# Softmax maxima 12 slots ahead instead of 16, and the routed experts two at a time over sixteen turns, in a fused two-layer kernel

## The chip, the cores and the metric

One NeuronCore of a Trainium2 chip runs the whole program. The metric is device time in microseconds (us) from start to end of one execution, as the median of several runs. Engines are named as the profile names them: PE (matrix), PEld (its weight loads), DVE (vector), ACT (scalar), POOL (GpSimd), SP (the engine that here only issues DMAs).

## The reference

Two layers over 16 batches of 512 tokens of 128 features. What matters here:

```python
# layer 0: test-time memory (a small MLP trained chunk by chunk), then
xc   = causal_conv3(layernorm(x)) ; q, k, v = xc @ wqkv          # full attention
att0 = softmax(q k^T / sqrt(8)) v         # 16 heads of 8 features, 512 x 512 each
x1   = layernorm(att0 @ wo + x)           # "z" below; then a dense mixture of 8 experts
# layer 1
a    = causal_attention(x)                # 16 heads of 8
b    = causal_attention(conv3(a))         # a second one on its result
# routed experts: 32, top 8 of a token, at most 128 tokens each
h    = silu(gate(row)) * up(row) ; out[token] += weight * down(h)
```

A softmax subtracts its row's maximum; the kernel takes the maximum of a row first, and computes the scores a second time with it subtracted.

## The kernel before

**Stages.** The memory's learning runs to about 357 us; then "attend0", whose tiles begin with c_ (to about 1112 us); then the mixture (a_, to 2192 us); then "layer1", whose tiles begin with b_ (to the end), with the routed experts (r_) spread over its first turns.

**An attention turn.** The class Attention handles one attention of one batch per turn p: 16 turns in attend0, 32 in layer1 (first and second attention of a batch take turns). A turn has SLOTS = 16 slots, G = 4 groups of heads by T = 4 tiles of queries; in layer1 a tile needs only the keys up to its own, so its slots get shorter in fours. In slot s of turn p:

- PE computes the scores of (p, s) (L1447, in layer1 also the mask L1454), from operand rows qa and ka. Rows of qa hold minus the row's maximum, so that the product is already shifted;
- ACT takes the exponentials (L1565);
- PE multiplies the exponentials of an earlier slot with the values (L1478);
- PE computes scores without the shift for the maxima of the *next* turn (L1415, mask L1421), and DVE reduces them (L1624, 128x1024 in, 128x2 out, two for a slot, one for a short one).

When some groups' maxima are there, a "shift" takes them into qa: PE transposes them (L1428), DVE makes two bf16 parts (L1632, L1633), SP sends two DMAs (L1393). The scores of these groups wait for them. A turn's shift has two parts, (p, 0) and (p, 1); moved() says in which slot each is made, EARLY how many groups the first part holds.

**Around it.** POOL splits q and k of a later turn in three bf16 parts (L1313 to L1319), and SP writes them to qa and ka with 12 or 6 DMAs (sync_rows, L1340 and L1343). The softmax sums travel by SP (spread L1365, context L1366), get their reciprocal on DVE (L1638, "inverse"), and go back (L1373, L1377, L1380), upon which DVE multiplies (L1385).

**Rings.** PE's results pass through two rings of PSUM banks in an order that plan() fixes: ring m (two pairs of banks) holds the maxima and most single jobs, ring s (three) the scores. A job in ring m can start only when the one two places ahead has been read. All engines run their instructions in program order.

**The single jobs.** attend0's last turn has no successor; in it the first batch of the mixture is prepared in slots that a table FIRST names: z in slot 2 (residual, two normalisations, the query; DVE L132 to L2003), x1 in slot 6 (DVE L2007), gate in 7, query in 8, hidden in 10, memory in 13. The class Routed takes Q = 4 experts at a time, a group to each of the first 8 turns: counting in LOCAL (slot 2), selecting in SELECT (slot 4; PE L2777, DVE L2835 to L2841), rows gathered, up and gate products in UP, silu in GATE (DVE L2847, L2848), HIDDEN, DOWN, and an indirect DMA of POOL adds the result to a sum. Batches that are finished before all experts are through are parked (PARKED = 3), and their output is written later.

Of the kernel before, what the change touches and what calls it, by code (L numbers as in the profile page):

```python
# [9 lines left out]
ACT = mybir.ActivationFunctionType  # L10
ALU = mybir.AluOpType
X = mybir.AxisListType.X

P = 128
# [3 lines left out]
T = S // P  # L18
NT = NB * T
# [7 lines left out]
G = 4  # L27
# [5 lines left out]
F1 = 96  # L33
CAP = 128
ROWS = N + CAP
# [132 lines left out]
SLOTS = G * T  # L168
BUFFERS = 3
SPREAD = 16  # L170
PAIRS = G // 2
EARLY = G - 1
GAP = 16
# [944 lines left out]
class Attention:  # L1118
# [115 lines left out]
    def moved(self, p, s):  # L1234

        jobs = [(p, 1)] if s == 0 else [(p + 1, 0)] if s == EARLY * T else []
        return [job for job in jobs if self.has(job[0])]

    def inverting(self, p, s):
# [17 lines left out]
    def plan(self, more_m, more_s, turns):  # L1257


        for p in turns:  # L1260
            for s in range(SLOTS):
                if self.has(p):
                    for j in self.heads(s, 0):
                        self.s.add("exp", p, s, j)
                jobs = [("shift", *job) for job in self.moved(p, s)] + more_m(p, s)
                maxima = [("max", p + 1, s, u) for u in self.units(s)] if self.has(p + 1) else []
                for job in maxima[0:1] + jobs + maxima[1:]:
                    self.m.add(*job)
                for job in more_s(p, s):
                    self.s.add(*job)  # L1270
                if self.has(p) and 1 in self.units(s):
                    for j in self.heads(s, 1):
                        self.s.add("exp", p, s, j)
# [209 lines left out]
    def tensor_turn(self, pe, p, extra_s, extra_m):  # L1483
        for s in range(SLOTS):
            t = s % T
# [5 lines left out]
            def maxima(u):  # L1491
                if self.has(p + 1) and u in self.units(s):
                    self.tensor_maxima(pe, p + 1, s, u)

# [114 lines left out]
    def vector_maxima(self, dve, p, s, u):  # L1609
        g, t = divmod(s, T)  # L1610
        if self.causal:
            t = T - 1 - t
        w = (t + 1) * P if self.causal else S
        if g < EARLY:
            out = self.maxima[0][:, :].rearrange("p (f g u t) -> p f g u t", f=2, g=EARLY, u=2)[:, :, g]
        else:
            out = self.maxima[1][:, :].rearrange("p (f u t) -> p f u t", f=2, u=2)
        src = self.m.bank("max", p, s, u)
        if self.together(s):
            out, src = out[:, :, :, t], src[:, :, 0:2 * w].rearrange("p f (u k) -> p f u k", u=2)  # L1620
        else:
            out, src = out[:, :, u, t], src[:, :, 0:w]
        dve.wait_ge(self.m.ready, self.m.count("max", p, s, u))
        self.nc.vector.reduce_max(out, src, X).then_inc(self.m.free, 1)  # L1624
# [24 lines left out]
    def vector_turn(self, dve, p, own, extra):  # L1649
        for s in range(SLOTS):  # L1650
            units = self.units(s) if self.has(p + 1) else ()
            for u in units[0:1]:
                self.vector_maxima(dve, p + 1, s, u)
            for job in self.moved(p, s):
                self.vector_shift(dve, *job, own)
            for job in self.inverting(p, s):
                if self.causal or job != (len(self.turns) - 1, PAIRS - 1):
                    self.vector_inverse(dve, *job)
            extra(p, s)
            for u in units[1:]:  # L1660
                self.vector_maxima(dve, p + 1, s, u)

# [70 lines left out]
def attend0(nc, ctx0, head, kept, ctxt, K, ps, bank, a, x, mem, memw1t, consts_loaded, learned, xnt_d, xc_d, ctxt_d):  # L1733
# [4 lines left out]
    with ExitStack() as ctx:  # L1738
# [50 lines left out]
        with nc.Block() as block:  # L1789
            @block.sync  # L1790
            def _(sp):
# [3 lines left out]
                for p in range(-2, NB):  # L1795
                    if att.has(p):
                        att.sync_shift(sp, p, 1)
                    if att.has(p - 1):
# [6 lines left out]
                    if att.has(p - 1):  # L1805
                        att.sync_inverse(sp, p - 1, PAIRS - 1)
                        sp.wait_ge(att.normalised, p)
                        sp.dma_start(ctxt_d[(p - 1) * P:p * P, :], ctxt[:, :]).then_inc(ctxt_stored, 16)
# [825 lines left out]

Q = 4
GROUPS = E1 // Q


class Routed:
# [4 lines left out]

    LOCAL, SELECT, ROWS, UP, GATE, HIDDEN, DOWN = 2, 4, 1, (5, 6), 7, 9, 11
    TOTAL, BEFORE, INCLUDED = 9, 10, 11
# [79 lines left out]
    def tensor_s(self, pe, p, s):  # L2726
        nc, ring = self.nc, self.att.s
        for job in self.jobs_s(p, s):
# [9 lines left out]
            if job[0] == "local":  # L2738
                g = job[1]
                total = self.total[:, g * Q:(g + 1) * Q].unsqueeze(2).broadcast_to([P, Q, P])  # L2740
                nc.tensor.matmul(out[0:NT, :], self.earlier[:, :], total, start=True, stop=False)
                for q in range(Q):
                    last = nc.tensor.matmul(out[0:NT, q * P:(q + 1) * P], self.chosen[:, g * Q + q, :], self.upto[:, :], start=False, stop=q == Q - 1)
# [40 lines left out]
    def scalar(self, act, p, s):  # L2784
        nc, ring = self.nc, self.att.s
        for job in self.jobs_s(p, s):
# [7 lines left out]
            if job[0] == "local":  # L2794
                if job[1]:
                    act.wait_ge(self.att.m.ready, self.att.m.count("sel", job[1] - 1))
                last = nc.scalar.activation(self.count[:, :], src[0:NT, :], ACT.Copy)
            if job[0] == "rt":
                last = nc.scalar.activation(self.rt[:, :], src, ACT.Copy)
            if job[0] == "gu":  # L2800
# [4 lines left out]
            if job[0] == "ht":  # L2805
                last = nc.scalar.activation(self.ht[:, :], src[0:F1, :], ACT.Copy, scale=0.5)
            if job[0] == "eo":
# [10 lines left out]
    def vector(self, dve, p, s, own):  # L2818
# [13 lines left out]
        if g is not None and s == self.SELECT:  # L2832
            src = m_ring.bank("sel", g)
            dve.wait_ge(m_ring.ready, m_ring.count("sel", g))
            nc.vector.tensor_scalar(self.tiles[:, :], src[:, 1, 0:Q], float(P), None, ALU.mult)  # L2835
            nc.vector.tensor_scalar(self.below[:, :, :], src[:, 0, :].rearrange("p (q k) -> p q k", q=Q), self.K("slot"), None, ALU.is_le
                                    ).then_inc(m_ring.free, 1)
# [5 lines left out]
        if g is not None and s == self.GATE:  # L2843
            dve.wait_ge(s_ring.free, s_ring.count("gu", g, 1))
            if g:
                dve.wait_ge(s_ring.ready, s_ring.count("ht", g - 1))
            own.done(nc.vector.scalar_tensor_tensor(self.th[:, :, :], self.th[:, :, :], 1.0, self.gu[:, :, 0:F1], ALU.add, ALU.mult))  # L2847
            nc.vector.tensor_tensor(self.h[:, :, :], self.th[:, :, :], self.gu[:, :, F1:2 * F1], ALU.mult).then_inc(self.h_ready, 1)  # L2848
# [58 lines left out]
FIRST_GROUP = 0  # L2907
PARKED = 3

# [7 lines left out]
def layer1(nc, ctx0, K, front, chosen, gate_up, down, table_d, sum_d, result):  # L2917
# [5 lines left out]
    with ExitStack() as ctx:  # L2923
# [18 lines left out]
        routed = Routed(ctx, ctx0, nc, K, att, FIRST_GROUP, chosen, gate_up, down, table_d, sum_d)  # L2942
        whole_turn = FIRST_GROUP + GROUPS + 1
        outputs = {}
# [46 lines left out]
        with nc.Block() as block:  # L2991
            @block.sync
            def _(sp):
                sp.wait_ge(att.m.ready, att.m.count("v", 0))
                front.load_x(sp, 2)
                for p in range(-1, len(turns) + 1):
                    if att.has(p - 1):
                        att.sync_spread(sp, p - 1, PAIRS - 1)
                    if att.has(p):
                        att.sync_shift(sp, p, 1)  # L3000
                    routed.sync_weights(sp, p)
# [10 lines left out]
                    if att.has(p - 1):  # L3012
                        att.sync_inverse(sp, p - 1, PAIRS - 1)
                    if att.has(p):
                        att.sync_spread(sp, p, 0)
                    if att.has(p + 2):
# [309 lines left out]
```

## Time and profile before

| | |
|---|---|
| median of 3 runs | 3385.29 us (3382.37 to 3389.59) |
| profiled execution, own time | 3388.66 us |
| its span | 3386.8 us |
| mean granted PE clock | 0.975 |
| PE busy | 3115.7 us, 92% |
| DVE busy | 2534.1 us, 75% |
| ACT busy | 2057.6 us, 61% |
| POOL busy | 877.2 us, 26% |

The span is what the trace covers; the execution's own time is 1.86 us more. All stretches below are counted in us from the span's start, in this execution. Busy shares are means over stages whose limits differ: a change is judged where it acts.

### The profile page before, as it was taken

The page shows a single profiled execution, that of the slowest core. Times are in us where ns is not written, and L with a number is a line of the kernel's source. Part 1 is how long each engine was busy: PE and PEld are TensorE (multiplying, and loading weights), DVE is VectorE, ACT ScalarE, POOL GpSimd, SP SyncE. Part 2 cuts the span into 40 slices and gives each one's busy share as a digit, 9 for nine tenths or more (in the row PEclk, how much of TensorE's full clock was granted, in tenths as well). Part 3 has the DMA queues.
Part 4 walks back from the last instruction along what each step waited for, and adds up shares of the span by engine and source line. Part 5 has one row for each costly group of instructions (what it writes and reads, how often), then busy time and mean ns, then how long its engine had stood idle before and what let it go on. Part 6 is the DMA issues. An engine that isn't in the chain of part 4 may idle for free. (4 is left out here: it accounts for less than half of the span.)

```text
span 3386.8 us, 83147 instructions
## 1 busy us (share of the span) xinstructions
PE 3115.7 (92%) x33099; PEld 1852.8 (55%) x33099; DVE 2534.1 (75%) x5014; ACT 2057.6 (61%) x4153; POOL 877.2 (26%) x783
## 2 busy tenths in 40 slices
PE   6887799999999999999999999789999999999997
PEld 5776322222223677777777777545555554555554
DVE  5777788888887476677667766677887877778874
ACT  6775288888888443333434334247777666776776
POOL 3322311111111322342233224224342211111110
PEclk9998799999999999999999999889999999999999
DMA  4100122222221110010001101223333232222222
GB/s 142 36 20 4 54 80 83 78 81 84 81 75 53 34 30 30 23 33 29 29 23 33 35 23 30 49 77 95 90 93 81 79 98 86 80 78 80 84 61 67
DMA packets 234976, 204.91 MB, mean 61 GB/s; under 512 B 74340, under 2 KB 190852, under 8 KB 234500
## 3 DMA queue, kind: packets, MB, share of 16 engines
q1 hardware_dynamic: 228484, 195.50, 20.1%
q0 software_dynamic: 6144, 4.72, 1.0%
q8 instruction: 224, 3.67, 0.5%
q14 instruction: 124, 1.02, 0.1%
HBM read 73.61 MB, written 59.39 MB: 39 GB/s over the span
## 5 line engine op out<-in xcount | busy, mean ns | idle before, releaser
L1624 DVE TENSOR_REDUCE b_maxima<-psum 128x2 f32<-128x1024 f32 (+3 forms) x768 | 779.8, 1041 | 227.0 <-PE psum L1421 216.9
L1565 ACT ACTIVATE b_prob<-psum 128x512 f32<-128x512 f32 (+2 forms) x1536 | 725.5, 526 | 298.4 <-PE psum L1454 292.0
L1624 DVE TENSOR_REDUCE c_maxima<-psum 128x2 f32<-128x1024 f32 x512 | 592.5, 1213 | 58.1 <-PE psum L1415 57.3
L1565 ACT ACTIVATE c_prob<-psum 128x512 f32<-128x512 f32 x1024 | 547.2, 600 | 113.9 <-PE psum L1447 97.3
L2378 PEld LDWEIGHTS psum<-consts_layer,a_hid 128*128 128x128 f32 x4096 | 477.5, 192 | 53.8 <-issue 53.6
L2368 PE MATMUL psum<-a_x1t,consts_layer 128*128 128x512 f32 x1024 | 462.1, 595 | 20.8 <-ACT a_hid L2438 13.8
L2378 PE MATMUL psum<-consts_layer,a_hid 128*128 128x128 f32 x4096 | 479.0, 275 | 0.0
L2438 ACT ACTIVATE a_hid<-psum,consts_layer 128x512 f32<-128x512 f32 x512 | 347.0, 687 | 197.2 <-PE psum L2368 190.5
L1478 PE MATMUL psum<-b_prob,b_v 128*32 128x128 f32 (+3 forms) x5632 | 398.4, 371 | 15.9 <-ACT b_c L1572 15.4
L1447 PE MATMUL psum<-b_qa,b_ka 64*128 64x512 bf16 (+3 forms) x2048 | 344.2, 303 | 40.1 <-ACT b_prob L1565 26.0
L2605 DVE SCALAR_TENSOR_TENSOR a_acc<-psum,a_gprob,a_acc 128x128 f32<-128x128 f32 x512 | 143.7, 343 | 261.1 <-PE psum L2378 233.1
L1415 PE MATMUL psum<-b_ka,b_qa 62*128 62x512 bf16 (+3 forms) x2048 | 305.3, 306 | 27.5 <-DVE b_maxima L1624 17.6
L1478 PE MATMUL psum<-c_prob,c_v 128*32 128x256 f32 (+1 forms) x3840 | 320.2, 405 | 1.7 <-ACT c_prob L1565 0.6
L2368 PEld LDWEIGHTS psum<-a_x1t,consts_layer 128*128 128x128 f32 x1024 | 187.1, 191 | 223.7 <-issue 197.3
L1447 PEld LDWEIGHTS psum<-b_qa,b_ka 64*128 64x128 bf16 x2048 | 122.3, 93 | 292.9 <-ACT b_prob L1565 209.1
L1454 PE MATMUL psum<-b_kmask,b_pick 64*128 64x64 bf16 x4096 | 242.5, 190 | 0.0
L1447 PE MATMUL psum<-c_qa,c_ka 64*128 64x512 bf16 x1024 | 218.8, 388 | 19.1 <-ACT c_prob L1565 18.7
L1421 PEld LDWEIGHTS psum<-b_qmask,b_pick 64*128 64x128 bf16 x4096 | 201.0, 97 | 51.0 <-issue 5.2
L1421 PE MATMUL psum<-b_qmask,b_pick 64*128 64x64 bf16 x4096 | 226.7, 191 | 0.0
L1415 PE MATMUL psum<-c_ka,c_qa 62*128 62x512 bf16 x1024 | 209.4, 388 | 18.2 <-DVE c_maxima L1624 17.7
L1454 PEld LDWEIGHTS psum<-b_kmask,b_pick 64*128 64x128 bf16 x4096 | 186.0, 95 | 44.4 <-issue 1.3
L1478 PEld LDWEIGHTS psum<-c_prob,c_v 128*32 128x32 f32 x3840 | 75.6, 108 | 204.2 <-issue 111.5
(407 smaller groups left out, 4200.7 us busy)
## 6 DMA issues: line engine op xcount, KB each, us to landing
b_qa<-b_part SPq DMA_DIRECT2D x192, 128.0 KB
b_context<-b_c SPq DMA_DIRECT2D x64, 256.0 KB, 2.1
c_qa<-c_part SPq DMA_DIRECT2D x96, 128.0 KB, 2.5
c_ka<-c_part SPq DMA_DIRECT2D x96, 128.0 KB, 2.6
b_ka<-b_part SPq DMA_DIRECT2D x96, 128.0 KB
c_context<-c_c SPq DMA_DIRECT2D x32, 256.0 KB, 2.1
b_scale<-b_inverse SPq DMA_DIRECT2D x64, 128.0 KB
b_unscaled<-b_context SPq DMA_DIRECT2D x64, 128.0 KB
```

The lines of the kernel that those rows point to most:

```text
L1415: last = nc.tensor.matmul(out[:, half, k0:k0 + w], qa[rows, hh, t * P:(t + 1) * P], ka[rows, hh, 0:w], start=True, stop=not self.causal)
L1421: last = nc.tensor.matmul(out[:, half, k1:k1 + HALF], self.pick[n][rows, :], self.qmask[rows, :], start=False, stop=n == 1)
L1447: last = nc.tensor.matmul(outs[half][:, k0:k0 + w], ka[rows, hh, t * P:(t + 1) * P], qa[rows, hh, q0:S], start=True, stop=not self.causal)
L1454: last = nc.tensor.matmul(outs[half][:, k0 + n * HALF:k0 + (n + 1) * HALF], self.pick[n][rows, :], self.kmask[rows, :], start=False, stop= ...
L1478: product = nc.tensor.matmul(self.acc[32 * j:32 * (j + 1), q0:q1], self.values(p)[:, t, column:column + 32], self.prob[:, s % 2, j, q0:q1] ...
L1565: self.nc.scalar.activation(out, src, ACT.Exp, scale=SCALE).then_inc(self.s.free, 1)
L1624: self.nc.vector.reduce_max(out, src, X).then_inc(self.m.free, 1)
L2368: nc.tensor.matmul(bank[4 + u % 3], K("up0", e * F0 + f * P, P), x1t[n][:, :], start=True, stop=True).then_inc(up_ready.sem, 1)
L2378: last = nc.tensor.matmul(tiled(2 + e % 2)[:, t, :], hid[:, e % 2, f, t * P:(t + 1) * P], K("down0", (e * FC + f) * D, D), start=f == 0, s ...
L2438: nc.scalar.activation(hid[:, e % 2, f, :], bank[4 + u % 3], ACT.Relu, bias=K("upb0", u, 1)).then_inc(hid_ready.sem, 1)
L2605: last = nc.vector.scalar_tensor_tensor(acc[n][:, t, :], tiled(2 + e % 2)[:, t, :], gprob[n][:, t, e:e + 1], acc[n][:, t, :], ALU.mult, AL ...
```

## The change

- EARLY goes from 3 groups to 2, and the maxima run LEAD = 12 slots ahead instead of 16. Slot s of turn p now makes the maxima of slot s + 12 counted on: for s = 0 to 3 the last four of its own turn, for s = 4 to 15 the first twelve of the next turn. The program's first maxima thus stand in slot 4 of turn -1, and four slots of maxima fall into the last turn of each attention stage.
- shift (p, 1) is made in slot 4 of turn p instead of slot 0, and first needed by the scores of slot 8 instead of slot 12. shift (p + 1, 0) stays in slot 12, with 32 partitions instead of 48.
- On SP, shift (p, 1) stands behind the inverse's DMAs of the turn before instead of ahead of them.
- Routed: Q = 2 in 16 groups over 16 turns instead of 4 in 8; SELECT in slot 5, UP in 6, GATE in 10, HIDDEN in 11, DOWN in 13. PARKED is 7.
- The table FIRST isn't touched.

The diff, cut to its core:

```diff
-EARLY = G - 1
+EARLY = G // 2
+LEAD = SLOTS - T
@@ Attention
     def moved(self, p, s):
-        jobs = [(p, 1)] if s == 0 else [(p + 1, 0)] if s == EARLY * T else []
+        jobs = [(p, 1)] if s == SLOTS - LEAD else [(p + 1, 0)] if s == EARLY * T + SLOTS - LEAD else []
         return [job for job in jobs if self.has(job[0])]
+
+    def leading(self, p, s):
+
+        return divmod(p * SLOTS + s + LEAD, SLOTS)
@@ plan
-                maxima = [("max", p + 1, s, u) for u in self.units(s)] if self.has(p + 1) else []
+                maxima = [("max", *self.leading(p, s), u) for u in self.units(s)] if self.has(self.leading(p, s)[0]) else []
                 for job in maxima[0:1] + jobs + maxima[1:]:
@@ vector_turn (tensor_turn alike)
-            units = self.units(s) if self.has(p + 1) else ()
+            q, r = self.leading(p, s)
+            units = self.units(r) if self.has(q) else ()
@@ sync, layer1 (attend0 alike)
-                    if att.has(p):
-                        att.sync_shift(sp, p, 1)
                     routed.sync_weights(sp, p)
...
                         att.sync_inverse(sp, p - 1, PAIRS - 1)
                     if att.has(p):
+                        att.sync_shift(sp, p, 1)
                         att.sync_spread(sp, p, 0)
@@ Routed
-Q = 4
+Q = 2
-    LOCAL, SELECT, ROWS, UP, GATE, HIDDEN, DOWN = 2, 4, 1, (5, 6), 7, 9, 11
+    LOCAL, SELECT, ROWS, UP, GATE, HIDDEN, DOWN = 2, 5, 1, (6,), 10, 11, 13
@@ layer1
-PARKED = 3
+PARKED = 7
-        whole_turn = FIRST_GROUP + GROUPS + 1
+        whole_turn = FIRST_GROUP + GROUPS
```

**Place 1: DVE in attend0's last turn, end of the z job** (a_q and c_rstd are z's; c_spread is the inverse; a_x1t is the job x1). Before:

```order
L122 SCALAR_TENSOR_TENSOR c_rstd<-c_tmp,c_rstd 128x4
L2003 SCALAR_TENSOR_TENSOR a_q<-a_q,c_rstd,consts_shared 128x128 x4
L1638 RECIPROCAL c_spread<-c_spread 128x32
L2007 TENSOR_SCALAR a_x1t<-psum,consts_layer 128x512
L2011 TENSOR_TENSOR c_gsm<-psum,consts_layer 128x32
```

Now:

```order
L122 SCALAR_TENSOR_TENSOR c_rstd<-c_tmp,c_rstd 128x4
L2009 SCALAR_TENSOR_TENSOR a_q<-a_q,c_rstd,consts_shared 128x128 x4
L1628 TENSOR_REDUCE c_maxima<-psum 128x2 x2
L1642 RECIPROCAL c_spread<-c_spread 128x32
L1628 TENSOR_REDUCE c_maxima<-psum 128x2
L1636 TENSOR_SCALAR c_shift<-psum 32x128
L1637 SCALAR_TENSOR_TENSOR c_shift<-psum,c_shift 32x128
L2013 TENSOR_SCALAR a_x1t<-psum,consts_layer 128x512
```

The last three reduces of the kernel's own last maxima, and the shift made of them, now stand behind the whole z job; before, all maxima and the shift stood ahead of it.

**Place 2: DVE in turn 4 of layer1, from slot 3 or 4 on** (r_ tiles are the selection of a group of experts, b_ctxt or b_unscaled the scaling of a finished attention). Before:

```order
L1624 TENSOR_REDUCE b_maxima<-psum 128x2x2
L1638 RECIPROCAL b_spread<-b_spread 128x32
L1624 TENSOR_REDUCE b_maxima<-psum 128x2
L2835 TENSOR_SCALAR r_tiles<-psum 128x4
L2836 TENSOR_SCALAR r_below<-psum,consts_layer 128x512
L2839 TENSOR_REDUCE r_slot<-r_below 128x4
L2840 TENSOR_TENSOR r_slot<-r_tiles,r_slot 128x4
L2841 TENSOR_SCALAR r_index<-r_slot,consts_layer 128x4
L1624 TENSOR_REDUCE b_maxima<-psum 128x2 x3
L1624 TENSOR_REDUCE b_maxima<-psum 128x2x2
L1385 TENSOR_TENSOR b_ctxt<-b_unscaled,b_scale 128x512
```

Now:

```order
L1636 TENSOR_SCALAR b_shift<-psum 32x128
L1637 SCALAR_TENSOR_TENSOR b_shift<-psum,b_shift 32x128
L1628 TENSOR_REDUCE b_maxima<-psum 128x2 x2
L2841 TENSOR_SCALAR r_tiles<-psum 128x2
L2842 TENSOR_SCALAR r_below<-psum,consts_layer 128x256
L2845 TENSOR_REDUCE r_slot<-r_below 128x2
L2846 TENSOR_TENSOR r_slot<-r_tiles,r_slot 128x2
L2847 TENSOR_SCALAR r_index<-r_slot,consts_layer 128x2
L1628 TENSOR_REDUCE b_maxima<-psum 128x2
L1628 TENSOR_REDUCE b_maxima<-psum 128x2x2
L1390 TENSOR_TENSOR b_ctxt<-b_unscaled,b_scale 128x512
```

The shift's two instructions have moved from the turn's start into slot 4, and the selection, half as wide, stands two reduces behind it, a slot later than before.

**Place 3: SP at the start of turn 4 of layer1** (r_wgu and r_wdn are the weights of a group of experts, b_qa the operand rows that the scores wait for). Before:

```order
L1365 DMA b_spread<-b_c 128x1x32
L1366 DMA b_context<-b_c 128x512
L1393 DMA b_qa<-b_shift 2x8x128 x2
L2903 DMA r_wgu<-gate_up 128x768
L2904 DMA r_wdn<-down 96x512
L1373 DMA b_inverse<-b_spread 128x32
L1377 DMA b_scale<-b_inverse 64x1x512
L1380 DMA b_unscaled<-b_context 64x1x512
```

Now:

```order
L1370 DMA b_spread<-b_c 128x1x32
L1371 DMA b_context<-b_c 128x512
L2909 DMA r_wgu<-gate_up 128x384
L2910 DMA r_wdn<-down 96x256
L1378 DMA b_inverse<-b_spread 128x32
L1382 DMA b_scale<-b_inverse 64x1x512
L1385 DMA b_unscaled<-b_context 64x1x512
L1398 DMA b_qa<-b_shift 2x16x128 x2
```

The shift's two DMAs now follow the three of the inverse, each with 16 blocks instead of 8.

## Rows read from the trace of the kernel before

**Rows 1.** The page's first part: busy time of each engine.
```profile
PE 3115.7 (92%) x33099; PEld 1852.8 (55%) x33099; DVE 2534.1 (75%) x5014; ACT 2057.6 (61%) x4153; POOL 877.2 (26%) x783
```
**Rows 2.** PE's waits in layer1's turns 0 to 16: total us, times, longest.
```profile
PE psum L1447 <- DMA b_qa<-b_shift: 11.6, 6, 4.6
PE psum L1415 <- DVE b_maxima L1624: 10.3, 10, 2.9
```
**Rows 3.** Stretches: length, each engine's busy us, granted clock, DMA share, GB/s.
```profile
2226.50:2863.20 636.70, 587.63 (x10110) 333.74 (x10106) 508.94 (x623) 448.13 (x971) 188.54 (x182) 0.99 0.34 88
2390.60:2430.60 40.00, 37.31 (x625) 21.93 (x623) 34.34 (x44) 28.65 (x64) 17.50 (x17) 1.00 0.43 106
2430.60:2468.20 37.60, 36.24 (x615) 21.38 (x611) 30.41 (x42) 28.33 (x63) 14.59 (x17) 1.00 0.36 85
...
2226.50:2270.80 44.30, 35.32 (x585) 19.05 (x581) 33.54 (x40) 24.79 (x52) 10.60 (x9) 0.92 0.31 78
...
2653.50:2686.70 33.20, 31.61 (x576) 17.55 (x578) 26.16 (x31) 24.35 (x52) 6.10 (x6) 1.00 0.27 76
2686.70:2722.70 36.00, 32.45 (x588) 17.86 (x585) 29.24 (x34) 24.55 (x52) 7.61 (x5) 1.00 0.36 100
```
**Rows 4.** Timeline of SP before attend0's first scores: start, us, instruction.
```profile
393.11 0.59 SPq L1343 DMA_DIRECT2D c_ka<-c_part  x1
395.28 1.15 SPq L1393 DMA_DIRECT2D c_qa<-c_shift  x2
```
**Rows 5.** Timeline of DVE there.
```profile
381.10 13.66 DVE L1624 TENSOR_REDUCE c_maxima<-psum 128x2 f32<-128x1024 f32 x12
```
**Rows 6.** Timeline of PE: attend0's first scores.
```profile
401.67 0.63 PE L1447 MATMUL psum<-c_qa,c_ka 64*128 64x512 bf16 x2
```
**Rows 7.** Timeline of DVE in attend0's last turn, the z job and the stage's end.
```profile
1069.47 0.89 DVE L132 BATCH_NORM_STATS2 c_stats<-psum 128x6 f32<-128x128 f32 x4 [7.10 <-PE psum L1907]
...
1074.28 0.68 DVE L1996 SCALAR_TENSOR_TENSOR a_q<-a_q,psum 128x512 f32<-128x512 f32 x1
...
1078.63 1.14 DVE L2003 SCALAR_TENSOR_TENSOR a_q<-a_q,c_rstd,consts_shared 128x128 f32<-128x128 f32 x4
...
1111.19 0.69 DVE L2038 TENSOR_TENSOR a_q<-a_q,c_rest 128x512 f32<-128x512 f32 x1
```
**Rows 8.** Timeline of PE ahead of layer1's first scores.
```profile
2202.99 2.07 PE L3072 MATMUL psum<-b_xt,consts_layer 128*128 128x512 f32 x2
...
2220.20 0.61 PE L1415 MATMUL psum<-b_ka,b_qa 62*128 62x512 bf16 x2 [0.52 <-DVE b_maxima L1624]
...
2226.50 0.62 PE L1447 MATMUL psum<-b_qa,b_ka 64*128 64x512 bf16 x2
```
**Rows 9.** Timeline of POOL there: the last memset, and the first part.
```profile
2201.11 0.20 POOL L1303 MEMSET b_v<- 128x64 f32 x1
2205.86 1.04 POOL L1313 CAST b_part<-b_qk 128x1024 bf16<-128x1024 f32 x1 [4.54 <-ACT b_qk L3116]
```
**Rows 10.** Timeline of DVE, selection in turn 4 of layer1, then in turn 5.
```profile
2404.02 2.04 DVE L2840 TENSOR_TENSOR r_slot<-r_tiles,r_slot 128x4 f32<-128x4 f32 x1
...
2443.19 0.16 DVE L2840 TENSOR_TENSOR r_slot<-r_tiles,r_slot 128x4 f32<-128x4 f32 x1
```
**Rows 11.** Timeline of POOL in turn 4.
```profile
2403.91 2.13 POOL L1315 TENSOR_TENSOR b_rest<-b_qk,b_part 128x1024 f32<-128x1024 f32 x1
...
2407.22 2.12 POOL L1319 TENSOR_TENSOR b_part<-b_rest,b_part 128x1024 bf16<-128x1024 f32 x1
```
**Rows 12.** Timeline of PE: turn 3's first scores, and a wait in turn 4.
```profile
2351.65 0.39 PE L1447 MATMUL psum<-b_qa,b_ka 64*128 64x512 bf16 x2 [3.18 <-DMA b_qa<-b_shift]
...
2408.35 0.34 PE L1415 MATMUL psum<-b_ka,b_qa 62*128 62x384 bf16 x2 [2.03 <-DVE b_maxima L1624]
```
**Rows 13.** Timeline of SP: turn 3's shift, and turn 5's last inverse DMA.
```profile
2348.88 1.14 SPq L1393 DMA_DIRECT2D b_qa<-b_shift  x2
...
2442.95 0.61 SPq L1380 DMA_DIRECT2D b_unscaled<-b_context  x1
```

More of the change, by code:

```diff
@@ L1491, in maxima @@
             def maxima(u):
-                if self.has(p + 1) and u in self.units(s):
-                    self.tensor_maxima(pe, p + 1, s, u)
+                q, r = self.leading(p, s)
+                if self.has(q) and u in self.units(r):
+                    self.tensor_maxima(pe, q, r, u)
             def values(slots, half=None):
@@ L1613, in vector_maxima @@
         w = (t + 1) * P if self.causal else S
[L1614 to L1617, printed above, removed]
+        n, g = divmod(g, EARLY)
+        out = self.maxima[n][:, :].rearrange("p (f g u t) -> p f g u t", f=2, g=EARLY, u=2)[:, :, g]
         src = self.m.bank("max", p, s, u)
@@ L1650, in vector_turn @@
         for s in range(SLOTS):
-            units = self.units(s) if self.has(p + 1) else ()
+            q, r = self.leading(p, s)
+            units = self.units(r) if self.has(q) else ()
             for u in units[0:1]:
-                self.vector_maxima(dve, p + 1, s, u)
+                self.vector_maxima(dve, q, r, u)
             for job in self.moved(p, s):
@@ L1660, in vector_turn @@
             for u in units[1:]:
-                self.vector_maxima(dve, p + 1, s, u)
+                self.vector_maxima(dve, q, r, u)
 @dataclass
@@ L1806, in _ @@
                         att.sync_inverse(sp, p - 1, PAIRS - 1)
+                    if att.has(p):
+                        att.sync_shift(sp, p, 1)
+                    if att.has(p - 1):
                         sp.wait_ge(att.normalised, p)
@@ L2740, in tensor_s @@
                 total = self.total[:, g * Q:(g + 1) * Q].unsqueeze(2).broadcast_to([P, Q, P])
-                nc.tensor.matmul(out[0:NT, :], self.earlier[:, :], total, start=True, stop=False)
+                nc.tensor.matmul(out[0:NT, 0:Q * P], self.earlier[:, :], total, start=True, stop=False)
                 for q in range(Q):
@@ L2796, in scalar @@
                     act.wait_ge(self.att.m.ready, self.att.m.count("sel", job[1] - 1))
-                last = nc.scalar.activation(self.count[:, :], src[0:NT, :], ACT.Copy)
+                last = nc.scalar.activation(self.count[:, :], src[0:NT, 0:Q * P], ACT.Copy)
             if job[0] == "rt":
-                last = nc.scalar.activation(self.rt[:, :], src, ACT.Copy)
+                last = nc.scalar.activation(self.rt[:, :], src[:, 0:Q * P], ACT.Copy)
             if job[0] == "gu":
@@ L2805, in scalar @@
             if job[0] == "ht":
-                last = nc.scalar.activation(self.ht[:, :], src[0:F1, :], ACT.Copy, scale=0.5)
+                last = nc.scalar.activation(self.ht[:, :], src[0:F1, 0:Q * P], ACT.Copy, scale=0.5)
             if job[0] == "eo":
@@ L2835, in vector @@
             nc.vector.tensor_scalar(self.tiles[:, :], src[:, 1, 0:Q], float(P), None, ALU.mult)
-            nc.vector.tensor_scalar(self.below[:, :, :], src[:, 0, :].rearrange("p (q k) -> p q k", q=Q), self.K("slot"), None, ALU.is_le
+            nc.vector.tensor_scalar(self.below[:, :, :], src[:, 0, 0:Q * P].rearrange("p (q k) -> p q k", q=Q), self.K("slot"), None, ALU.is_le
                                     ).then_inc(m_ring.free, 1)
@@ L2843, in vector @@
         if g is not None and s == self.GATE:
-            dve.wait_ge(s_ring.free, s_ring.count("gu", g, 1))
+            dve.wait_ge(s_ring.free, s_ring.count("gu", g, len(self.UP) - 1))
             if g:
@@ L2998, in _ @@
                         att.sync_spread(sp, p - 1, PAIRS - 1)
-                    if att.has(p):
-                        att.sync_shift(sp, p, 1)
                     routed.sync_weights(sp, p)
@@ L3014, in _ @@
                     if att.has(p):
+                        att.sync_shift(sp, p, 1)
                         att.sync_spread(sp, p, 0)
```

## The prediction

> **What bounds the kernel now.** I read the page first: PE is busy 92% of the span, DVE 75%, ACT 61% [rows 1]. So the time is PE's work plus what PE waits for, and the question is which waits this change removes and which it makes. PE's waits in layer1's turns 0 to 16 come next: 11.6 us in 6 waits for the shift's DMA, 10.3 us in 10 waits for a bank that DVE's maxima hold [rows 2]. Then the stretches show what a turn costs: 40.0 us for an even turn with a group of four experts (PE busy 37.31), 37.6 for an odd one (36.24), 36.0 and 33.2 for the same kinds without experts (32.45 and 31.61), 636.7 us for turns 0 to 16 together [rows 3]. Last, the timelines of three places where nothing overlaps well: the starts of both attention stages, where the first scores wait for the maxima of a whole turn [rows 4 to 6, 8, 9], and attend0's last turn [rows 7].
>
> What a measurement can tell of this kernel is about 0.2%, 6.8 us; terms below that size decide only together.
>
> **1. Start of attend0.** Now sixteen slots of maxima must be through before the first scores at 401.67 [rows 6]. DVE bounds them: twelve reduces take 13.66 us, 1.14 each [rows 5]. Four slots less are eight reduces, 9.1 us; that would put the scores at 392.6. But the shift of the first groups can't be sent before SP has issued the next batch's rows, the last of which ends at 393.11 + 0.59 = 393.70 [rows 4]. From the issue of a shift to the scores that wait for it I take turn 3 of layer1, where PE stood waiting: issued at 2348.88, scores at 2351.65, 2.8 us [rows 12, 13]. That gives 396.5 to 396.7: **-5.0 us** (bounds -3, if the shift lands later, and -9, if the rows finish earlier).
>
> **2. attend0's last turn.** Here the change adds. Before, this turn had no maxima, and z's 10.3 us on DVE, from 1069.47 to 1078.63 + 1.14 = 1079.77, lay beside scores and exponentials [rows 7]. Now slots 0 to 3 carry the turn's own last maxima, and z stays in slot 2: on DVE three reduces and the shift stand behind z's whole chain, and ring m has two places. (a) The second job behind z needs z's bank, which DVE has read only at 1074.28 + 0.68 = 1074.96, 5.5 us after the chain began [rows 7]; PE has about 1.4 us of scores and values to put there: a wait of 4.1. (b) The next needs the reduce that stands behind the chain's end: 1079.77 + 1.14 = 1080.91, 5.95 us after (a)'s release, less some 1.25 of PE's work between: 4.7. (c) The last reduce before the transposition: about 0.9. (d) The maxima and transposition themselves: 0.7. Together 10.4 us. Everything behind stands too, since PE keeps program order: the exponentials, x1, the gate, the memory read, whose last DVE instruction at 1111.19 lies ahead of the mixture [rows 7]. So the lag is carried into the total. In turn 0 of layer1, which has the longest waits, the mean granted clock was 0.92, where the turns without long waits show 1.00 [rows 3]; the lower of the clock's two levels (1.2 GHz instead of 2.4) doubles a matmul's time, so I add 1.1 us. **+11.5 us** (bounds +7 and +15).
>
> The Trainium skill (TensorE: Matmul & The Clock Gate, "HAM oscillation — how this bites in real kernels") tells of kernels whose clock falls at each long wait for data and has to come back; by that rule each of waits (a) and (b) may be followed by a stretch at half clock, which speaks against this change.
>
> **3. Start of layer1.** The same with shorter slots. The last four slots' maxima run from 2220.20 to the first scores at 2226.50 [rows 8]. Is SP in the way again? K of batch 1 stands behind four slots of maxima, at 2202.99 [rows 8]; POOL's first split follows at 2205.86 and SP's rows follow that. Now K stands behind none of them, and POOL is free from 2201.11 + 0.20 on [rows 9]. So the split starts some 4.5 us earlier and the rows end that much earlier, ahead of the shift. Here the maxima alone decide: 6.3 us less the transposition and its neighbours, **-5.6 us** (bounds -3 and -6.5).
>
> **4. Turns 0 to 16 of layer1.** The experts' work is the same, only spread: per turn the mean of both kinds. Odd: PE busy (36.24 + 31.61)/2 = 33.9, plus the 1.5 us that both kinds wait [rows 3], 35.4. Even: (37.31 + 32.45)/2 = 34.9 [rows 3]. What an even turn waits is the disputed part. The selection's short L2840 took 2.04 us in turn 4 and 0.16 in turn 5 [rows 10]; in turn 4 it ended with POOL's L1315, which ran from 2403.91 to 2406.04 [rows 11]. PE then stood 2.03 us for a bank [rows 12]. In the new order the selection comes a slot later. From the start of slot 4 its L2840 falls at +6.3 us, where POOL's second cast ended at about +7.0 in turn 4; L2841 then meets POOL's last subtraction (2407.22 to 2409.34) [rows 11]. DVE loses about 3 us, and PE, with three reduces queued behind, 0.4 + 1.55 = 1.95, as much as now. With 1.3 for the rest an even turn is 34.9 + 3.3 = 38.2. Turn 0 and turn 2, with longer waits now, I put at 41.2 and 39.7, turns 1 and 3 a microsecond over 35.4. Sum: 8 x 35.4 + 2 + 41.2 + 39.7 + 6 x 38.2 + 38.2 for turn 16 = 633.5 against 636.7: **-3.2 us** (bounds -6 and +2). It is small because the stall with POOL now comes in eight even turns, half as much work beside it.
>
> The Trainium skill (SBUF — State Buffer, "Who interferes with whom") says that DVE and GpSimd take a shared pair of ports in turn, that an instruction of DVE with two inputs in SBUF is blocked for the whole of GpSimd's, and that a reduce never is. By that rule, the trace agrees: L2840 waited, with 2.04 against 0.16 us.
>
> **5. The rest.** Steady turns of attend0: the transposition moves from slot 0 to slot 4, with nothing late behind it: 0. Very last turn: four slots of maxima and a transposition where PE is idle enough to take most: +0.5. Parking seven batches moves DVE's and SP's work, which nobody waits for: 0; uncovered it would cost about a DVE instruction of 0.7 us per batch. Shift (p, 1) behind the inverse on SP: the inverse's last DMA in turn 5 was issued by 2442.95 + 0.61 = 2443.56 [rows 13]; plus 2.8 it lands at 2446.4, while slot 8 begins at about half of the turn, 2448.8: 0.
>
> Sum: -5.0 + 11.5 - 5.6 - 3.2 + 0.5 = **-1.8 us**. The profiled execution took 3388.66 us, so 3386.9; its time lies 3.4 over the median of the three runs, so I predict a median of **3383.5 us**.
>
> **The rivals.**
>
> *A. The selection slips past POOL (faster).* If DVE gets to L2840 0.3 us before POOL's second cast, or POOL is late by the same, the 1.95 us of wait fall away in seven even turns: -13.7, to about 3369.8. For it: the margin is small and half-width instructions are shorter. Against it: DVE has the shift's two instructions ahead now. 0.20.
>
> *B. The shift is late for slot 8 (slower).* It waits behind the inverse's round trip, its slack in odd turns is 2448.8 - 2446.4 = 2.4 us. The point from which it decides is an inverse that takes 2.4 us longer, or even turns where DVE's shift comes after the selection; at about 1 us in 20 of 32 turns it gives +20: 3403. Against it: in turn 5 there is slack. 0.12.
>
> *C. z costs more (slower).* If the exponentials' ring is drained as well, and the clock stays at the lower level for the rest of slots 4 to 7, another 8 to 10 us: 3392. 0.10.
>
> *D. z costs little (faster).* If the turn, with ACT as its bound, makes up for half of the lag behind slot 4: 3375 to 3377. 0.06. The forecast itself has 0.52, with its own range 3377 to 3390.
>
> **The numbers.** Faster by over 0.2% (below 3378.5): A, D and a tail of the forecast, 0.29. Slower (above 3392.1): B, half of C and a tail, 0.23. Within: 0.48. The range reaches to A on one side and between C and B on the other, 3368 to 3398.
>
> **What would show it.** First scores of attend0 near 396.7; two waits of PE of 4 to 5 us in attend0's last turn, on z's bank and on the maxima, and the mixture's start some 6.5 us later than now; layer1's first scores 5.6 us sooner after its first maxima; even turns near 38.2 and odd ones near 35.4; L2846 at about 1 us and L2847 at about 2. The prediction is wrong if the last turn's lag isn't carried, if the even turns differ by 2 us in either direction, or if scores in slot 8 wait for the shift.

## The result, and the profile after

The changed kernel takes 3417.05 us (median of 3 runs, 3415.9 to 3417.92) against 3385.29: ratio 1.0093, 95% interval 1.0079 to 1.0107. It is slower, and outside the range given. In later runs the changed kernel took the same, 3418.0, but the kernel before took 3411 to 3419 in three sets, each on its own chip, and where both were timed side by side they were equal (1.0004, 0.9995 to 1.0013). Both facts need a cause; the second is taken up with the runs E7 and R1.

The page of the kernel after, and its stretches (columns as in [rows 3]): turns 0 to 16 of layer1, an even turn, an odd one, an even one further on.

```profile
span 3414.1 us, 83367 instructions
...
PE 3132.5 (92%) x33107; PEld 1861.1 (55%) x33107; DVE 2548.1 (75%) x5094; ACT 2060.0 (60%) x4177; POOL 883.7 (26%) x795
```

```profile
2224.50:2883.40 658.90, 604.03 (x10117) 339.41 (x10112) 522.67 (x703) 450.61 (x995) 175.93 (x178) 0.97 0.31 80
...
2384.10:2424.20 40.10, 36.68 (x605) 20.92 (x601) 32.66 (x44) 26.68 (x59) 12.11 (x11) 0.96 0.34 88
2424.20:2460.95 36.75, 34.57 (x597) 19.58 (x593) 29.07 (x42) 26.55 (x60) 9.30 (x11) 1.00 0.28 72
...
2536.90:2578.30 41.40, 38.02 (x605) 21.00 (x601) 32.72 (x44) 26.84 (x60) 12.10 (x11) 0.92 0.33 87
```

The span grew by 27.3 us, and 22.2 of them lie in these seventeen turns (658.9 for 636.7 in [rows 3]). An odd turn is at 36.75 where 35.4 was forecast, an even one at 40.1 and 41.4 where 38.2 was. Note the granted clock: 0.96 and 0.92 in the even turns, 0.97 over the whole, where [rows 3] have 1.00 and 0.99. PE is busy 16.4 us more for the same results, and idle 5.8 more.

PE's waits in the same turns (total, times, longest), beside [rows 2]:

```profile
PE psum L1420 <- DVE b_maxima L1628: 15.5, 8, 2.7
...
PE psum L2767 <- DVE r_h L2854: 10.1, 16, 1.0
PE psum L1452 <- DMA b_qa<-b_shift: 6.8, 3, 4.3
```

The second is new: in slot 11 PE transposes the silu's result, which DVE has made only in slot 10; 16 waits, 10.1 us. The wait for the shift's DMA went down (11.6 to 6.8), though a shift that is made later leaves fewer slots to hide it behind.

The two starts and attend0's last turn. SP at attend0's first scores; then PE there, in attend0's last turn, and at the starts of the mixture and of layer1:

```profile
390.69 0.59 SPq L1348 DMA_DIRECT2D c_ka<-c_part  x1
391.32 1.14 SPq L1398 DMA_DIRECT2D c_qa<-c_shift  x2
```
```profile
393.73 0.61 PE L1452 MATMUL psum<-c_qa,c_ka 64*128 64x512 bf16 x2 [3.64 <-DMA c_qa<-c_shift]
...
1067.04 0.61 PE L1420 MATMUL psum<-c_ka,c_qa 62*128 62x512 bf16 x2 [4.21 <-DVE a_q L2002]
...
1072.97 0.61 PE L1420 MATMUL psum<-c_ka,c_qa 62*128 62x512 bf16 x2 [3.78 <-DVE c_maxima L1628]
...
1116.86 9.15 PE L2374 MATMUL psum<-a_x1t,consts_layer 128*128 128x512 f32 x16 [7.00 <-PEq L1794]
...
2198.34 2.07 PE L3073 MATMUL psum<-b_xt,consts_layer 128*128 128x512 f32 x2 [6.44 <-POOL b_cpad L3044]
...
2224.46 0.62 PE L1452 MATMUL psum<-b_qa,b_ka 64*128 64x512 bf16 x2
```

Scores start at 393.73 for 401.67 [rows 6]: -7.9, and they wait for the shift's DMA, which SP issues right behind the rows, as reasoned; the rows themselves now end 2.4 us sooner than in [rows 4]. But so does all that lies ahead of them: POOL's very first split for attend0, in the stage of the memory, before and after:

```profile
331.26 1.26 POOL L261 CAST c_part<-c_qk 128x1024 bf16<-128x1024 f32 x1 [2.47 <-ACT c_qk L245]
```
```profile
328.81 1.27 POOL L262 CAST c_part<-c_qk 128x1024 bf16<-128x1024 f32 x1 [2.47 <-ACT c_qk L246]
```

The change doesn't touch that stage, and over all profiles of this document this split starts anywhere from 327.6 to 331.3, with either lead. Counted from it the first scores come after 64.9 us instead of 70.4: 5.5 of the 7.9 us are attend0's own, 2.4 came from ahead of it.

In the last turn stand the two waits that were forecast, 4.21 on z's bank (4.1) and 3.78 on the reduce behind z's chain (4.7). For the turn's length (55.4, under E4) and layer1's start, two lines of before, a stretch and PE's first maxima of layer1:

```profile
1060.50:1105.00 44.50, 41.33 (x365) 16.16 (x365) 20.00 (x64) 34.69 (x68) 19.34 (x17) 1.00 0.14 47
```
```profile
2194.65 0.61 PE L1415 MATMUL psum<-b_ka,b_qa 62*128 62x512 bf16 x2 [6.48 <-POOL b_cpad L3039]
```

layer1 goes from its first matmul to its first scores in 26.1 us (2198.34 to 2224.46), where it took 31.9 (2194.65 to 2226.50): 5.7 less.

### The profile page after: what moved, and what is told of

The parts are those of the page before. It is cut to its first block and busy times, and to the rows that moved or that the text cites. A ratio compares the mean times of both kernels' runs of the same rounds, so it can differ in the third digit from the quotient of the medians.

```text
span 3414.1 us, 83367 instructions
## 1 busy us (share of the span) xinstructions
PE 3132.5 (92%) x33107; PEld 1861.1 (55%) x33107; DVE 2548.1 (75%) x5094; ACT 2060.0 (60%) x4177; POOL 883.7 (26%) x795
## 5 line engine op out<-in xcount | busy, mean ns | idle before, releaser
L1420 PE MATMUL psum<-c_ka,c_qa 62*128 62x512 bf16 x1024 | 209.7, 387 | 22.7 <-DVE c_maxima L1628 17.9
L1452 PEld LDWEIGHTS psum<-c_qa,c_ka 64*128 64x128 bf16 x1024 | 56.0, 93 | 242.7 <-ACT c_prob L1571 195.3
```

Of the source, the lines that this page charges most:

```text
L1420: last = nc.tensor.matmul(out[:, half, k0:k0 + w], qa[rows, hh, t * P:(t + 1) * P], ka[rows, hh, 0:w], start=True, stop=not self.causal)
L1452: last = nc.tensor.matmul(outs[half][:, k0:k0 + w], ka[rows, hh, t * P:(t + 1) * P], qa[rows, hh, q0:S], start=True, stop=not self.causal)
```

## The experiments

All were timed in 5 rounds against the kernel before on the same chip (three chips, one for each set of four). Read them by the ratio, or by the kernel beside them in their set.

**Set 1. E1: the lead of 12 alone.** The experts as before; in short (whole_turn, too, is FIRST_GROUP + GROUPS + 1 again):
```diff
-Q = 2            PARKED = 7     SELECT 5, UP (6,), GATE 10, HIDDEN 11, DOWN 13
+Q = 4            PARKED = 3     SELECT 4, UP (5, 6), GATE 7, HIDDEN 9, DOWN 11
```


> The changed kernel with the experts as before (four at a time in eight turns, old slots, three batches parked): the lead of 12 slots alone. Theory P (the loss is in the experts' slicing): layer1's turns 0 to 16 take what they took before, 636.7 us within 5, and the whole is -8.0 (attend0's start) +10.9 (its last turn) +1.1 (mixture) -5.7 (layer1's start) +3.1 (last turn), about +1.4: 3387. Theory L (the shorter lead itself makes layer1's turns wait: the shift behind the inverse, maxima nearer to their scores): turns 0 to 16 near 655, the whole near 3407.

Measured 3420.61, ratio 1.0022 (1.0012 to 1.0032). Turns 0 to 7 took 355.5 us instead of 320.6, which seemed to speak for theory L. But the kernel before itself took 3413.27 there, 28 us over its first time, with a lead of 16: most of the 35 us isn't the lead's. By the ratio the lead alone costs 7.3 us here where theory P has 1.4; how much of the other 6 is the lead and how much the chip, this run doesn't tell (E8 and E9 do, for two experts at a time). In turns 8 to 16, which have no experts here, E1 takes 312.5 us, the kernel before 316.1 and, in R1, 313.3: there the shorter lead costs nothing.

**E2: the experts alone**, the kernel before with Q = 2 and the new slots, lead 16.

> The kernel before with only the experts changed (two at a time in sixteen turns, new slots, seven batches parked), lead of 16 slots. Theory P: turns 0 to 16 at 655 to 659 in place of 636.7, some 4 us more in turns 18 to 22; whole near 3410. Theory L: turns 0 to 16 near 637, whole within 5 us of 3385. In theory P the wait of PE for the silu of DVE (some 0.98 us in each odd turn) is there, in theory L it may be too, but the even turns are back at 38.

Measured 3416.88, ratio 1.0014 (1.0003 to 1.0026). Its turns 0 to 16:
```profile
2222.40:2883.70 661.30, 603.12 (x10118) 338.90 (x10112) 525.59 (x703) 450.79 (x995) 176.35 (x179) 0.97 0.31 80
```
661.3 us, with the same PE busy time (603.12 for 604.03) and the same waits as the changed kernel (16.4 for DVE's maxima, 10.1 for the silu): the loss in these turns comes with the experts two at a time in their new slots, whatever the lead. Theory P holds for them, though they are 2 us over its 659 and the whole is 7 us over its 3410 (4 in the profiled execution).

**E3: silu one slot sooner.**
```diff
-    ... GATE, HIDDEN, DOWN = ... 10, 11, 13
+    ... GATE, HIDDEN, DOWN = ... 9, 11, 13
```


> The changed kernel with the experts' silu on DVE one slot sooner (GATE 9 instead of 10), nothing else. PE's transposition of its result in slot 11 now waits 10.1 us in 16 turns. If that wait is a real part of the loss, eight odd turns become 0.98 us shorter (36.7 to 35.7) and the whole is some 8 us less: 3409. If it only moves (to the exponentials, or to the result's copy), the odd turns stay at 36.7 and the whole at 3417.

Measured 3405.43, ratio 0.9980 (0.9968 to 0.9991). An odd turn of it:
```profile
2424.60:2460.30 35.70, 34.49 (x597) 19.55 (x593) 29.43 (x43) 26.42 (x59) 9.34 (x11) 1.00 0.29 74
```
35.7 for 36.75, turns 0 to 16 648.2 for 658.9, and the wait of L2767 is gone from PE's list. That wait was real, and worth what it said. (The changed kernel wasn't in this set; with its 3417 to 3418 elsewhere the gain is some 12 us, for 8 expected.)

**E4: z behind the last maxima.**
```diff
-FIRST = {2: "z", 6: "x1", 7: "gate", 8: "query", 10: "hidden", 13: "memory"}
+FIRST = {4: "z", 7: "x1", 8: "gate", 9: "query", 11: "hidden", 14: "memory"}
```


> The changed kernel with the mixture's first batch moved: z in slot 4 of attend0's last turn, behind the last maxima, and x1, gate, query, hidden, memory one slot later each. If the 10.9 us that this turn has grown by are the maxima that queue behind z's chain, the two waits of 4.2 and 3.8 us are gone, the turn is near 45.5, the mixture starts 8 to 10 us sooner (1107 to 1109), and the whole is 3407 to 3409. Rival: the lag is a matter of the last maxima themselves (DVE and ring places in slots 0 to 3), the turn stays over 52, and the whole is within 3 us of 3417.

Measured 3411.84, ratio 0.9997 (0.9987 to 1.0007). The last turn, after and in E4:
```profile
1052.20:1107.60 55.40, 44.71 (x381) 16.42 (x380) 28.59 (x72) 34.96 (x68) 19.96 (x18) 0.91 0.12 37
```
```profile
1053.80:1102.70 48.90, 43.34 (x381) 16.43 (x380) 28.15 (x67) 34.96 (x68) 18.29 (x16) 0.97 0.13 43
```
```profile
1080.35 1.03 PE L1921 MATMUL psum<-consts_layer,a_x1t 128*128 128x8 f32 x8 [3.38 <-DVE a_x1t L2013]
```
6.5 us less, not 10: the two waits are gone, but the gate in slot 8 now waits 3.38 us for x1, which DVE makes behind z's chain (the third line, PE in E4). So it was z's place that held the maxima. The mixture starts 4.9 us sooner than in the changed kernel (1111.97 for 1116.86), not 8 to 10, and the whole missed its 3407 to 3409: against the 3417 to 3418 of the changed kernel elsewhere it gained 5 to 6 us.

**Set 2. R1 and R2: both kernels again, on one chip.**

> The kernel before, unchanged, for its profile beside the other runs on the same chip. In the last set of runs it took 3413 there, 28 us over its time at first. Theory C (a second cost that comes and goes with the chip: with four experts at a time, layer1's turns 0 to 7 wait in slots 4 to 8 for things that the profile lays to nothing on the core): on a chip where it takes 3413, its turns 0 to 7 together are near 350 instead of 320.6, and on one where it takes 3385 they are 320.6. Theory D (the lead of 12 makes those waits, and the chip is slower all over): turns 0 to 7 near 321 on either.

> The changed kernel, unchanged, beside the kernel before on the same chip. Where the kernel before takes 3385: ratio 1.009 again, theory C and D alike. Where it takes 3413: theory C says 3412 to 3418, ratio within 0.2% of 1, since two experts at a time don't have that cost; theory D says 1.009, 3445.

R1 3414.89 (ratio to the other runs of the same kernel 0.9991), R2 3418.0 (1.0004). R1's turns 0 to 7, and beside them one of its groups: POOL's four row gathers, and ACT.
```profile
2225.40:2570.70 345.30, 307.20 (x4880) 175.08 (x4876) 256.08 (x331) 224.59 (x493) 117.99 (x124) 0.97 0.34 84
```
```profile
2457.91 1.01 POOL L2876 DMA_INDIRECT r_row<-table,r_index  x1 [0.15 <-issue]
...
2461.76 0.94 POOL L2876 DMA_INDIRECT r_row<-table,r_index  x1 [0.30 <-issue]
```
```profile
2458.53 0.87 ACT L1565 ACTIVATE b_prob<-psum 128x384 f32<-128x384 f32 x2 [0.18 <-PE psum L1454]
2463.00 1.25 ACT L1565 ACTIVATE b_prob<-psum 128x512 f32<-128x512 f32 x2 [3.59 <-issue]
```
345.3 for the 320.6 of the first chip. ACT ended at 2459.40 and had its next scores from PE at 2459.6; it went on at 2463.00, 0.3 us behind the end of the fourth gather. The trace names no releaser for it ("issue"; for others of ACT's and DVE's idle times, 15.9 and 20.6 us in these turns, "remote"). In R2, with two gathers in a row, there are none. Theory C holds, D is out. (E1's 355.5 are 10 us over R1's 345.3, on another chip; that part has no cause here.)

**E5: selection in slot 7.**
```diff
-    LOCAL, SELECT, ROWS, ... = 2, 5, 1, ...
+    LOCAL, SELECT, ROWS, ... = 2, 7, 1, ...
```


> The changed kernel with the selection in slot 7 instead of 5, nothing else. In even turns POOL's split of q and k should be through by then. If DVE's block behind POOL is what makes the 1.84 us waits and the half clock that follows: L2846 and L2847 are short (0.16 and 0.23) in even turns too, these turns go from some 40.4 to 37.5 or 38.5, and the whole is 15 to 20 us under the changed kernel. Rival: the selection's place in ring m makes another wait in slot 7 or 8, beside v's; even turns stay over 40 and the whole within 4 us.

Measured 3397.43, ratio 0.9949 (0.9935 to 0.9962): 20.6 us under R2. DVE in turn 4, after (first fence) and in E5, and E5's turn 4 and turns 0 to 16:
```profile
2399.34 0.85 DVE L2846 TENSOR_TENSOR r_slot<-r_tiles,r_slot 128x2 f32<-128x2 f32 x1
2400.23 2.18 DVE L2847 TENSOR_SCALAR r_index<-r_slot,consts_layer 128x2 int32<-128x2 f32 x1
```
```profile
2400.10 0.16 DVE L2846 TENSOR_TENSOR r_slot<-r_tiles,r_slot 128x2 f32<-128x2 f32 x1
2400.29 0.23 DVE L2847 TENSOR_SCALAR r_index<-r_slot,consts_layer 128x2 int32<-128x2 f32 x1
```
```profile
2379.70:2417.40 37.70, 35.74 (x607) 19.86 (x605) 31.28 (x43) 26.95 (x59) 12.13 (x11) 1.00 0.36 93
...
2224.60:2866.10 641.50, 598.85 (x10118) 332.64 (x10116) 516.14 (x703) 452.42 (x995) 176.26 (x178) 0.99 0.32 82
```
R2's turns 0 to 16, for comparison:
```profile
2226.90:2891.10 664.20, 606.98 (x10118) 339.38 (x10114) 523.05 (x703) 450.92 (x995) 175.92 (x178) 0.97 0.31 79
```
Of the 22.7 us, 10.5 are PE's waits for the maxima's bank (15.5 to 5.0), 4.8 its waits for the bank of v behind them (5.6 to 0.8), and 8.1 PE's busy time (606.98 to 598.85), at a clock of 0.99 for 0.97; other waits grew by 0.7. To 15.3 us of waits the clock had added about half as much again.

**E6: all three repairs** (selection 7, silu 9, z as in E4).

> The changed kernel with all three repairs: silu a slot sooner, z behind the last maxima, selection in slot 7. If the three losses are apart from one another their gains add: 8 + 7 + 15 to 20, so 30 to 35 us under the changed kernel, and 3 to 8 us under the kernel before where that takes 3385, more where it takes 3413. If they share a cause (the lowered clock), less than 25.

Measured 3383.51, ratio 0.9901 (0.9886 to 0.9916): 34.5 under R2, where E3, E4 and E5 by themselves gave some 12, 5 to 6 and 20.6. The gains all but add, though two of the three were measured across chips. Turns 0 to 16 take 637.3 us, as in the kernel before.

**Set 3. E7: the kernel before, its gathers two by two.**
```diff
         for q in range(Q):
+            if q == Q // 2:
+                pool.wait_ge(self.gathered[g % 2], 16 * (g // 2 * Q + q))
             self.nc.gpsimd.indirect_dma_start(out=self.row[g % 2][:, q, :], ...
```


> The kernel before with one wait added on POOL: of a group's four row gathers, the third is issued only when the first two have landed. On the chips of the experiments the kernel before takes 3413 to 3419, on that of the result 3385; the added time stands in its turns 0 to 7 (345.3 for 320.6), where ACT and DVE idle 2 to 4 us beside the four gathers. Theory C1 (four indirect DMAs in a row are what holds them): turns 0 to 7 come down towards 321, the whole 15 to 25 us under the kernel before on the same chip. Theory C2 (the amount of gathered data or the chip's memory, not their being in a row): turns 0 to 7 stay over 340 and the whole within 4 us. Rival to both: the rows land later and are missed by the next turn's first product; slower.

Measured 3394.65, ratio 0.9955 (0.9943 to 0.9968), 16.6 us under the 3411.22 of the kernel before. Its turns 0 to 7, and a group's gathers:
```profile
2220.10:2549.20 329.10, 300.00 (x4882) 172.94 (x4878) 255.74 (x331) 223.54 (x493) 119.06 (x124) 0.97 0.36 88
```
```profile
2442.96 0.98 POOL L2878 DMA_INDIRECT r_row<-table,r_index  x1 [0.30 <-issue]
2446.63 1.31 POOL L2878 DMA_INDIRECT r_row<-table,r_index  x1 [2.69 <-DMA r_row<-table,r_index]
```
329.1 for 345.3 (R1's, on another chip; the kernel before has no profile on this one), with ACT's "remote" idle time gone and 2.1 us left of DVE's. Theory C1: the same data in the same turns, paced, costs less. The wait spaces the gathers and also keeps at most two of them under way; which of the two helps, E7 can't tell.

**E8: lead of 16 with the experts two at a time, selection 7, silu 9.**

> The lead of 16 slots of the kernel before, with the experts two at a time, selection in slot 7, silu in slot 9; the first batch's slots as before. It tells what the lead of 12 is worth by itself, beside the kernel with all three repairs (3383.5). By the parts measured so far (attend0's start 8.0, layer1's start 5.7, against 5 in attend0's last turn even with z moved, 1 in the mixture, 0.4 to 3 in the very last turn) the lead of 12 is worth 5 to 8 us: this one takes 3388 to 3392. If the shorter lead costs anything in steady turns that the views don't show, this one is equal or faster.

**E9: E6 with x1 in slot 8, gate 9, query 10, hidden 12, memory 14.**

> The kernel with all three repairs, and in attend0's last turn x1 in slot 8, gate 9, query 10, hidden 12, memory 14 (z stays in 4). There the gate waited for z's chain on DVE and slot 8 took 8.0 us. If that wait goes, the turn falls from 49.8 to about 45.5; the memory read comes in the same slot, so the mixture starts some 2 to 4 us sooner: 3380 to 3382. Rival: hidden and memory two slots apart instead of three wait for each other, and the gain is under 1.

E8 3388.13 (0.9933, 0.9921 to 0.9945), E9 3382.05 (0.9921, 0.9909 to 0.9933), both as expected. Their turns 0 to 16, E8 first:
```profile
2223.70:2860.30 636.60, 598.25 (x10118) 333.99 (x10114) 519.22 (x703) 450.65 (x995) 176.45 (x180) 0.99 0.32 83
```
```profile
2217.50:2854.40 636.90, 599.73 (x10118) 333.17 (x10116) 518.48 (x703) 450.73 (x995) 176.03 (x178) 0.99 0.32 82
```
In steady turns the lead brings and costs nothing. The best version is E9, but its gain over E8 is all that the lead of 12 brings, with attend0's last turn arranged for it: 6.1 us in the medians, 4 by the ratios, with intervals that overlap over half their length. The profiles put it where it was reasoned: attend0's start -3.2 (from POOL's first split), layer1's start -5.7, against +2.9 in attend0's last turn. That turn is 47.4 us, not 45.5; the gate still waits.

**E10: the kernel before with its selection in slot 7.**

> The kernel before with the selection in slot 7 instead of 4, nothing else. The block of DVE behind POOL in four even turns (waits of 2.0 to 2.9) should go: 8 to 10 us, plus the half clock that followed two of them, 3: whole 10 to 14 us less than the kernel before on the same chip. If it gains more than 20, the gathers' new place also took the stalls beside them away. Rival: four experts' gather now ends too late for the next turn's slot 1: slower.

Measured 3396.28, ratio 0.9960 (0.9948 to 0.9972): 14.9 us less, for 10 to 14 expected. One number in the kernel before is thus worth more than the lead. Its turns 0 to 7:
```profile
2224.30:2553.40 329.10, 300.72 (x4880) 173.71 (x4876) 248.98 (x332) 225.07 (x493) 121.89 (x124) 0.97 0.37 88
```
329.1 us, as in E7, with its four gathers still in a row, 0.30 us apart, but three slots later: ACT's and DVE's "remote" idle times are 2.8 and 5.1 us, for R1's 15.9 and 20.6. So four in a row don't cost the same everywhere, and how the 14.9 us divide between the block behind POOL and these stalls isn't shown.

## Why the prediction was wrong

**Right, with sizes.** Start of attend0: -7.9 measured, -5.0 forecast; -5.5 without the 2.4 us that came from ahead of the stage. I had taken SP's rows as fixed at 393.70, and they move with that stage. Even the 5.5 hangs on the run: with a lead of 16, the kernel before, R1 and E10 took 70.4 us from POOL's first split to the first scores, E2, E7 and E8 67.7 to 68.1, against 64.9 to 65.0 in all eight profiles with a lead of 12. The lead is worth 2.7 to 5.5 us here. attend0's last turn: 55.4 for 44.5, +10.9, forecast +11.5, with both waits where they were put; E4 shows z's place as the cause. The mixture's start came 2.6 us later, not 6.5, the 2.4 us from ahead being in it. layer1's start: -5.7, forecast -5.6. The very last turn: +0.4 in six other profiles of this lead, as forecast (+0.5), +1.6 in R2 and 3.1 in this one, at a mean clock of 0.89. Shift (p, 1) behind the inverse (rival B): no wait of PE for it in steady turns. At layer1's first scores the changed kernel is 2.0 us ahead (2224.46 against 2226.50 in [rows 8]), where steps 1 to 3 sum to 0.9 behind; 2.4 of these 2.9 us are the luck of the stage ahead. Up to there it was right.

**The step that failed is 4, turns 0 to 16: forecast -3.2, measured +22.2**, outside its own bounds of -6 and +2. Its parts, of which the last three make up the 25.4 us that were missed (10.1, about 11, 4 to 5):

- *DVE's block behind POOL.* L2846 and L2847 took 0.85 and 2.18 us (first fence of E5) where "about 1 and about 2" were forecast, and PE's wait behind them was 1.84 where I had 1.95. Right, and E5 removes it:

```profile
2403.33 0.23 PE L1420 MATMUL psum<-b_ka,b_qa 62*128 62x128 bf16 x2 [1.84 <-DVE b_maxima L1628]
```

- *The silu's wait.* I worked out an odd turn's waits as the mean of two turns of the kernel before, in which silu and its transposition stand two slots apart (GATE 7, HIDDEN 9). In the new table they are one apart (10 and 11). PE waits 0.97 us in turn 5, an odd one, and 10.1 in sixteen turns: E3.
- *Work that isn't halved.* PE is busy 34.57 us in an odd turn at full clock; half the experts' work gives 33.9. So 0.6 to 0.7 us a turn, about 11 in sixteen, come with a group whatever its size. No experiment was made for it, but with the selection's wait repaired it stays: in turns 0 to 16 of E5, E6, E8 and E9 PE is busy 598.3 to 600.6 us, 11 to 13 over the 587.63 of the kernel before, while they spend no more time at the lower clock than it does.
- *The clock.* I charged the lower level (1.2 GHz) to attend0's last turn alone. Adding up the stretches with a granted clock of 0.5, the changed kernel spent 36.6 us of turns 0 to 16 there, the kernel before 17.4: 19.2 more. It costs less than half of that, since PE's instructions don't all double with it (a pair of products of 512 columns takes 0.61 us for 0.39, four masks 0.32 for 0.22): E5 spent 23.8 us less there than the changed kernel and 30.6 less than R2, and was busy 5.2 and 8.1 us less. At that rate, about a quarter, the 19.2 us are an estimated 4 to 5 of the 16.4 us that PE is busier. That such a wait can bring it on stood in the trace before: in turn 4 one of 2.03 us had left the clock at 1.00 [rows 3, 12], and I took that for the rule, but turn 6 has the same wait and a clock of 0.96, 1.3 us more for it:

```profile
2485.96 0.34 PE L1415 MATMUL psum<-b_ka,b_qa 62*128 62x384 bf16 x2 [2.03 <-DVE b_maxima L1624]
```
```profile
2468.20:2509.50 41.30, 38.74 (x625) 22.82 (x623) 34.47 (x44) 28.65 (x64) 17.10 (x18) 0.96 0.41 103
```

**Turns 17 to 31** (to the last turn's scores), +6.9 where only the last turn's +0.5 was forecast:

```profile
2863.20:3370.20 507.00, 471.24 (x8441) 258.43 (x8441) 385.11 (x452) 363.68 (x774) 70.59 (x60) 1.00 0.26 75
```
```profile
2883.40:3397.30 513.90, 475.15 (x8493) 261.46 (x8489) 392.60 (x459) 363.64 (x775) 89.61 (x76) 0.99 0.28 81
```

3.1 of them lie in the last turn, the rest in turns 18 to 22. Seven batches are parked instead of three. From turn 17 to the end of the span the nine profiles with seven parked took 525.3 to 530.7 us, the five with three 520.9 to 525.2, so step 5, which put nothing there, left out some 4 us. But seven parked always came with experts two at a time; that the parking is the cause was not tried.

**The rivals.** None came. A (the selection slips past POOL) was priced at 13.7 us; E5, which moves the selection past POOL on purpose, gained 20.6.

**What stays open.** What holds ACT and DVE while POOL issues four indirect DMAs in a row, and why the kernel before shows none of it in the result's execution. The record names no chip for the result, and no chip was used in two sets, so that it is the chip, and not some other difference between the sets, is assumed. E7 shows that pacing them takes the cost away, E10 that another place takes most of it; the trace doesn't name what is waited for. Open, too, is when a wait brings the clock down.

## What to carry to other kernels

When work is cut into more pieces, don't take the new turn as the mean of the old ones: read in the new order the distance of every producer to its consumer, and charge each piece what it costs besides its size. A wait in the middle of a steady loop should be charged the slower clock behind it as a likely cost, above all if the loop meets it eight times. Before moving much, try the single slot: with the selection out of POOL's way the two versions gained 15 and 21 us. And before a gain at a stage's start is put down to a change, look whether the stage started at the same time: here 2.4 of 7.9 us came from ahead of it.

## What was not expected of the hardware

- Four indirect DMAs in a row on POOL (about 1 us each, 0.3 us apart) held ACT and DVE for up to 4.4 us at a time on two of the chips used for the later sets (profiles of R1 and E1; 345.3 and 355.5 us for turns 0 to 7), with no semaphore named, and not on the first (320.6). With a wait between the second and the third (1.8 to 2.7 us, E7) the idle time was all but gone (329.1), and with the four in a later slot most of it was (E10, 329.1). Two in a row showed none in R2, and 0.3 us at a time in E8 and E9 (0.9 and 1.3 us in all).
- The same wait doesn't always lower the clock. In the even turns 2 to 14 of the five profiles with the selection in slot 5 (the changed kernel, R2, E2, E3, E4) PE waits 1.84 us at the same place: in 25 of the 35 turns a stretch at 1.2 GHz follows, in 10 none. Of the three waits of 2.03 us in the kernel before one was followed by it. In E5, without the waits, no even turn from 2 to 14 has any.
